# Graph network in two layers on one core: edge counts in groups of two and three chunks instead of four, with Wk on a second queue and the w products moved to the end

## What is computed

```python
edge_index = jnp.stack([src, dst])            # 16384 edges, dst sorted, 1024 nodes, x is 1024x512 f32
h = jnp.maximum(_layernorm(x), 0.0)
# layer 0: attention along edges
q = h @ Wq + bq; k = h @ Wk + bk; v = h @ Wv + bv
adj = jnp.zeros((N, N)).at[src, dst].set(1.0)
a = q @ k.T / sqrt(512);  a = a * adj + (1.0 - adj) * -1e6
x = x + softmax(a) @ v
# layer 1: two aggregations over the edges (with loops), weights from degrees
h = jnp.maximum(_layernorm(x), 0.0)
h = agg(h @ W1 + b1)                          # segment_sum of dinv[src]*dinv[dst]*h[dst] into src
h = relu(gamma * (h - mean) * rsqrt(var + 1e-5) + beta)
x = x + agg(h @ W2 + b2)
```

## The kernel before

| window (in order) | 14 | 15 | 0 | 1 | 2 | 3 | 4 | 5 | 6 | 7 | 8 | 9 | 10 | 11 | 12 | 13 | sum |
|---|---|---|---|---|---|---|---|---|---|---|---|---|---|---|---|---|---|
| first chunk | 119 | 123 | 0 | 32 | 45 | 55 | 64 | 71 | 78 | 85 | 91 | 95 | 101 | 106 | 110 | 115 | |
| chunks touched | 5 | 5 | 33 | 14 | 11 | 10 | 8 | 8 | 8 | 7 | 5 | 7 | 5 | 5 | 6 | 5 | 142 |
| groups of 4, chunks done | 2, 8 | 2, 8 | 9, 36 | 4, 16 | 3, 12 | 3, 12 | 2, 8 | 2, 8 | 2, 8 | 2, 8 | 2, 8 | 2, 8 | 2, 8 | 2, 8 | 2, 8 | 2, 8 | 43, 172 |
| 2 and then threes, chunks done | 5 | 5 | 35 | 14 | 11 | 11 | 8 | 8 | 8 | 8 | 5 | 8 | 5 | 5 | 8 | 5 | 55, 149 |

## Time and profile before

### The profile page before, as it was taken

How to read it: one execution, slowest core, us unless ns; L and a number is a source line. 1 busy time by engine, 2 the same in 40 slices (tenths; PEclk the granted TensorE clock), 3 DMA queues, 4 the chain that set the end, 5 groups by cost and what they waited for, 6 DMA issues and landing times.

```text
span 318.9 us, 4799 instructions
## 1 busy us (share of the span) xinstructions
PE 302.8 (95%) x1358; PEld 234.0 (73%) x1358; DVE 214.7 (67%) x481; ACT 143.5 (45%) x245; POOL 55.8 (17%) x96
## 2 busy tenths in 40 slices
PE   4996999999999799999999999999999999999995
PEld 3874746656757378888888888888788888888884
DVE  4892999999999814796575764748634189367311
ACT  2884973544435453645445456437543024433000
POOL 4395120000000061002214212020210024200000
PEclk9998799999999989999999999999999999999999
DMA  6812320000320030953727154242204000000231
GB/s 232 310 31 82 88 97 34 2 1 0 134 66 0 0 69 0 230 84 83 122 57 154 33 132 80 54 82 49 51 16 67 2 0 2 0 0 1 78 121 66
DMA packets 42309, 21.64 MB, mean 68 GB/s; under 512 B 35760, under 2 KB 36016, under 8 KB 42288
## 3 DMA queue, kind: packets, MB, share of 16 engines
q1 hardware_dynamic: 42288, 21.38, 26.7%
HBM read 10.88 MB, written 2.10 MB: 41 GB/s over the span
## 4 chain that ended last, share of the span: by engine, by line
PE 70%; DVE 11%; issue 5%; POOL 4%; DVEq 3%; ACT 3%; DMA 2%; SPq 1%; ACTq 0%; POOLq 0%
PE ps L936 16%; PE ps L937 16%; PE ps L938 16%; PE ps L1180 9%; PE ps L1103 8%; DVE src_oh L662 5%; PE ps L1011 4%; DMA qk_raw<-L_gnn_Wq_in 2%; POOL drel_second L352 2%; DVEq L662 2%; DVE dst_oh L664 2%; POOL drel_first L352 1%; DVEq L657 1%; ACT T L419 0%; ACT T L425 0%
## 5 line engine op out<-in xcount | busy, mean ns | idle before, releaser
L662 DVE TENSOR_SCALAR src_oh<-iota,ecol 128x512 f16 x172 | 49.1, 345 | 2.6 <-issue 1.6
L1011 PE MATMUL ps<-src_oh,dst_oh 128*128 x172 | 42.1, 385 | 4.6 <-DVE dst_oh L664 4.6
L1011 PEld LDWEIGHTS ps<-src_oh,dst_oh 128*128 x172 | 18.5, 114 | 20.9 <-issue 9.4
L1103 PE MATMUL ps<-cnt,qh 128*128 128x512 f32 x128 | 30.1, 391 | 0.3 <-ACT cnt L532 0.3
L434 ACT ACTIVATE cnt<-ps 64x512 int16<-64x512 f32 x32 | 18.9, 591 | 25.1 <-PE ps L1016 24.7
L1180 PE MATMUL ps<-qh,cnt 128*128 128x512 f32 x128 | 29.3, 390 | 0.0
L1103 PEld LDWEIGHTS ps<-cnt,qh 128*128 128x128 f32 x128 | 23.9, 188 | 5.6 <-DVE qh L815 0.7
L1180 PEld LDWEIGHTS ps<-qh,cnt 128*128 128x128 f32 x128 | 24.0, 188 | 5.2 <-DVE vb L917 0.3
L938 PE MATMUL ps<-v,pT 128*128 128x512 f32 x64 | 25.0, 390 | 0.0
L936 PE MATMUL ps<-hT,qh 128*128 128x512 f32 x64 | 24.9, 389 | 0.0
L937 PE MATMUL ps<-v,pT 128*128 128x512 f32 x64 | 24.9, 389 | 0.0
(11 more groups left out here) (178 smaller groups left out, 667.6 us busy)
## 6 DMA issues: line engine op xcount, KB each, us to landing
xt<-x_in SPq DMA_DIRECT2D x16, 256.0 KB, 3.3
out<-xt SPq DMA_DIRECT2D x8, 256.0 KB, 2.0
qk_raw<-L_gnn_Wk_in SPq DMA_DIRECT2D x2, 512.0 KB, 4.3
qk_raw<-L_gnn_Wq_in SPq DMA_DIRECT2D x2, 512.0 KB, 6.8
wB_raw<-L_gnn_Wv_in SPq DMA_DIRECT2D x2, 512.0 KB, 8.7
wB_raw<-L_gnn_W_in SPq DMA_DIRECT2D x2, 512.0 KB, 3.8
w_raw<-L_gnn_W_in SPq DMA_DIRECT2D x2, 512.0 KB, 4.1
bias_row<-L_gnn_b_in SPq DMA_DIRECT2D x2, 256.0 KB, 3.9
```

The source lines that it names most:

```text
L662: dve.tensor_scalar(src_oh[:, bass.ds(slot, 1), j, :].rearrange("p a n -> p (a n)"), iota[:, :], ecol[:, bass.ds(c + j, 1)], None, ALU.is_ ...
L1011: m = pe.matmul(ps[:, i % 2, :], dst_oh[:, bass.ds(slot, 1), :, j].rearrange("p a n -> p (a n)"), src_oh[:, bass.ds(slot, 1), j, :].rearra ...
L1103: m = pe.matmul(bank(g), qh[:, d, a, c * P:(c + 1) * P], cnt[:, d, n * HALF:(n + 1) * HALF], start=(d == 0 and a == 1), stop=last)
```

## The change

Six edits: (1) a window's counts start with two chunks in a straight line (`LEAD = 2`), whose first matmul begins the bank anew, so that the matmul with zeros at the start goes; (2) the loop then takes three chunks a round (`UNROLL = 3`); (3) POOL does the coefficients of row blocks 2 and 3 right after those of 0 and 1, and the targets of most windows later; (4) ACT issues the two loads of Wk, SP only those of Wq; (5) `columns_of_biases` goes in four parts after i = 6, 7, 8, 9 instead of two; (6) item w is made before the last window, and the w products and `mask_level` come after it.

```diff
-UNROLL = 4
+LEAD = 2
+UNROLL = 3
+PAD = 4
+ROUNDS = NW * (2 + NCH // UNROLL)
...
-             [("q", 0, 1)], [("q", 0, 2), ("w", 0, 0)], [("q", 0, 3)], [], []]
+             [("q", 0, 1)], [("q", 0, 2)], [("q", 0, 3)], [], [("w", 0, 0)]]
...
@@ block.sync
-        for n, (w, name) in enumerate(((Wk, "Wk_in"), (Wq, "Wq_in"))):
...
+        for j in range(LOADS):
+            sp.dma_start(half_of_qk(Q, j), half_in_dram(Wq, j)).then_inc(S[f"Wq_in{j}"], 16)
...
@@ block.gpsimd
-        for i in range(4):
+        for i in range(3):
             targets_of(i)
         ln1(0)
-        for i in range(4, NW):
+        ln1(2)
+        for i in range(3, 8):
             targets_of(i)
-        for t in range(2, NT, 2):
-            ln1(t)
+        ln1(4)
+        ln1(6)
+        for i in range(8, NW):
+            targets_of(i)
...
@@ block.scalar
+        for j in range(LOADS):
+            act.dma_start(half_of_qk(K, j), half_in_dram(Wk, j)).then_inc(S[f"Wk_in{j}"], 16)
...
@@ block.vector
+        def chunks_of(i, c, count):
+
+            k = dve.snap(made, min_val=0, max_val=ROUNDS)
+            slot = k & (RING - 1)
+            dve.wait_ge(S["onehots_used"], k + 1)
+            for j in range(count):
+                dve.tensor_scalar(src_oh[:, bass.ds(slot, 1), j, :].rearrange("p a n -> p (a n)"), iota[:, :],
+                                  ecol[:, bass.ds(c + j, 1)], None, ALU.is_equal)
+            dve.tensor_tensor(dst_oh[:, bass.ds(slot, 1), :, 0:count].rearrange("p a n u -> p (a n) u"),
+                              iota_w[:, :, 0:count],
+                              drel(i)[:, bass.ds(c, count)].rearrange("p (o u) -> p o u", o=1).to_broadcast(
+                                  [P, P, count]), ALU.is_equal).then_inc(S["onehots"], 1)
+            dve.reg_add(made, made, 1)
+
         def onehots(i, bounds):
 
-            first, end = bounds & 255, bounds >> 8
+            first, end = bounds & (NCH - 1), bounds >> 8
             dve.wait_ge(S["drel_ready"], i + 1)
-            with dve.Fori(first, end, UNROLL) as c:
...
+            chunks_of(i, first, LEAD)
+            with dve.Fori(first + LEAD, end, UNROLL) as c:
+                chunks_of(i, c, UNROLL)
...
-            if i == 7:
-                columns_of_biases(K)
-            if i == 9:
-                columns_of_biases(Q)
-            if i == NW - 2:
-                mask_level(slice(0, KC))
+            if 6 <= i <= 9:
+                columns_of_biases(K if i < 8 else Q, (0, 1) if i % 2 == 0 else (2, 3))
         for i in range(NW - 2, NW):
             for item in ahead[i]:
                 lo_of(item)
+        mask_level(slice(0, KC))
...
@@ block.tensor
+        def chunks(i, count, first):
+
+            k = pe.snap(used, min_val=0, max_val=ROUNDS)
+            slot = k & (RING - 1)
+            pe.wait_ge(S["onehots"], k + 1)
+            for j in range(count):
+                m = pe.matmul(ps[:, i % 2, :], dst_oh[:, bass.ds(slot, 1), :, j].rearrange("p a n -> p (a n)"),
+                              src_oh[:, bass.ds(slot, 1), j, :].rearrange("p a n -> p (a n)"), start=first and j == 0,
+                              stop=False, skip_group_check=True)
+            m.then_inc(S["onehots_used"], 1)
+            pe.reg_add(used, used, 1)
+
         def counts(i, bounds):
 
             if i >= 2:
                 pe.wait_ge(S["c16"], 2 * (i - 1))
-            pe.matmul(ps[:, i % 2, 0:32], zerob[:, :], zerob[:, 0:32], start=True, stop=False, skip_group_check=True)
...
+            chunks(i, LEAD, True)
+            with pe.Fori(first + LEAD, end, UNROLL):
+                chunks(i, UNROLL, False)
```

More of the change, by code:

```diff
@@ L101, in gnn_kernel @@
     vb, iota_w, dcol, drel_first = shared([("vb", [P, 2, D], F32)],
-                                    [("iota_w", [P, 2 * WIN, UNROLL], F16), ("dcol", [P, NCH + UNROLL], F16),
-                                     ("drel_first", [P, NW // 2, NCH + UNROLL], F16)])
+                                    [("iota_w", [P, 2 * WIN, UNROLL], F16), ("dcol", [P, NCH + PAD], F16),
+                                     ("drel_first", [P, NW // 2, NCH + PAD], F16)])
     hold("region_vb", 4)
-    p16T, drel_second = shared([("p16T", [P, 2, NT, P], F16)], [("drel_second", [P, NW // 2, NCH + UNROLL], F16)])
+    p16T, drel_second = shared([("p16T", [P, 2, NT, P], F16)], [("drel_second", [P, NW // 2, NCH + PAD], F16)])
     hold("region_p16T", 4)
@@ L109, in gnn_kernel @@
     hold("region_dst_oh", 4)
-    ecol = sb("ecol", [P, NCH + UNROLL], F32)
+    ecol = sb("ecol", [P, NCH + PAD], F32)
     hnT, res, res_h = shared(
@@ L214, in weight_load @@
         return at[:, part, j * k:(j + 1) * k, :]
+    half_of_qk = lambda n, j: qk_raw[:, n, j * KC // LOADS:(j + 1) * KC // LOADS, :]
+    half_in_dram = lambda w, j: w.rearrange("(k p) n -> p k n", p=P)[:, j * KC // LOADS:(j + 1) * KC // LOADS, :]
     ACT_COUNTS, DVE_COUNTS = (0, 1, 2, 3), (4, 5, 6, 7)
@@ L267, in _ @@
         load_w(1)
-        sp.wait_ge(S["uw_ready"], 2)
+        sp.wait_ge(S["uw_ready"], 4)
         sp.dma_start(bias_row[:, 0, :], bv.rearrange("(o n) -> o n", o=1).to_broadcast([P, D])).then_inc(S["bias_in"], 16)
@@ L443, in hi_of @@
                 if item == ("q", 0, 0):
-                    act.wait_ge(S["uw_ready"], 2)
+                    act.wait_ge(S["uw_ready"], 4)
                 if item == ("q", 1, 0):
@@ L669, in columns_of_biases @@
-        def columns_of_biases(n):
-            if n == K:
+            chunks_of(i, first, LEAD)
+            with dve.Fori(first + LEAD, end, UNROLL) as c:
+                chunks_of(i, c, UNROLL)
+        def columns_of_biases(n, ks):
+            if (n, ks) == (K, (0, 1)):
                 dve.wait_ge(S["qk_bias_in"], 32)
-            for k in range(KC):
+            for k in ks:
                 ins = dve.scalar_tensor_tensor(out=qk_raw[:, n, k, :], in0=qk_raw[:, n, k, :], scalar=1.0,
@@ L676, in columns_of_biases @@
                                                accum_out=uw[:, n, k:k + 1])
-            if n == Q:
+            if (n, ks) == (Q, (2, 3)):
                 ins = dve.scalar_tensor_tensor(out=bias_row[:, 0, :], in0=bias_row[:, 0, :], scalar=1.0,
@@ L691, in mask_level @@
             if blocks.start == 0:
-                dve.wait_ge(S["uw_ready"], 2)
+                dve.wait_ge(S["uw_ready"], 4)
                 dve.wait_ge(S["item_lo"], nth(("w", 0, 0)))
@@ L968, in make @@
                 else:
-                    pe.wait_ge(S["uw_ready"], 2)
+                    pe.wait_ge(S["uw_ready"], 4)
                 for k in range(KC):
```

## The result

The changed kernel takes 311.6 us (median of 4, 311.3 to 311.82), the kernel before 320.37 on the same chip (4 runs): 8.8 us less, ratio 0.9727 with a 95% interval of 0.9706 to 0.9747. The forecast was 312.3 us, in a range of 306 to 317. The profiled execution of the changed kernel took 311.82 us, its span is 309.8 us.

The account below looks back on a forecast made before the run. DVE was taken to set the pace of the windows, its sequencer almost as slow as its engine, after a start held up by POOL. -5.8 - 2.2 - 0.4 = -8.4 us against 320.72 gives 312.3 us, range 306 to 317.

Parts of the forecast that it names:

- (a): Start up to DVE's first `src_oh` of w0: POOL's new order ends ACT's wait, 28.8 for 34.62, -5.8 us.
- I take 0, with 1 us either way: At the start, Wk's loads on ACT's queue: Wq maybe up to 1 us earlier, Wk's second half later; counted as 0.
- (b): The windows, from 34.62 to 110.42, where DVE sets the pace: 73.6 us for 75.8, -2.2 us.
- the rows: POOL's eight `drel_second` rows, now in w0 and w1, slow DVE's `src_oh` there: 0.7 us.
- rival (2): In the windows DVE's sequencer doesn't hold DVE back, 68.3 us: total 307.0, range 305 to 309.5; 17%.
- rival (3): In the windows `dst_oh` of three costs 0.47, 3.8 us more: total 316, range 315 to 318; 13%.
- my own rule: A window of r rounds lasts the larger of 1.9 + 1.16 r + 0.1 and 0.75 + 1.13 r + 0.6 per low part.
- rival (4): Each of POOL's eight rows shuts DVE out for its whole 0.74 to 0.78 us: total 316.5 to 318; 4%.
- (c): From 110.42 to `copy_predicated` at 121.81: one chunk less in the last round at the low clock, -0.4 us.
- Rival (5): PE's sparser rounds make the clock fall, 1.8 us each; more than five on the path give over 321.6; 3%.

Follow-up runs that it names:

- e2: The kernel before with POOL's new order alone: 315.68 us, ratio 0.9877.
- e6: The changed kernel with bias columns in two parts again and item w, its products and the mask level back among windows w10 to w13: 312.96 us.
- e5: The changed kernel itself measured once more as a yardstick: 311.36 us, ratio 0.9729 to the kernel before.
- e9: The changed kernel with each `src_oh` only 256 columns wide, with the same instructions on DVE: 308.25 us (a single run).
- e13: The kernel before with the new grouping alone, plus 12 matmuls of zeros on PE before its wait for LayerNorm of blocks 2 and 3: 316.97 us.
- e1: The changed kernel with Wk's two loads back on SP's queue: 311.18 us, ratio 0.9725 to the kernel before.
- e1b: The changed kernel with Wk's loads back on SP, measured again beside the changed kernel: 310.94 us, ratio 0.971 to the kernel before.
- e10: The changed kernel with POOL's `iota_w` moved behind `ident`, `iota` and `half_pow`, Wk still on ACT's queue: 311.72 us.
- e11: The changed kernel with Wk's loads back on SP and POOL's `iota_w` moved behind `ident`: 310.99 us.
- e3: The kernel before with the grouping alone (two chunks in a straight line, rounds of three, no zero matmul at the start): 318.81 us, ratio 0.997.
- e4: The changed kernel with POOL's old order: 318.03 us, ratio 0.994 to the kernel before.

## Why the prediction was right, step by step

**(a), -5.8 forecast, -3.83 found.** POOL's order did what was said: coefficients at 22.77 us, ACT without a wait. Two things ate 2 us. From m(0,0) to the first `src_oh` of w0 it is 17.9 us in all the kernels that have edits 1, 2 and 3 (17.88 to 17.95), where I had 28.8 - 11.41 = 17.4: the gap ahead of `src_oh` is 0.76 to 0.79 us, not 0.5, and the rest is spread. And m(0,0) itself was 1.43 us later in the profiled execution. The step that failed is "I take 0, with 1 us either way" for Wk's queue. I had looked only at Wk and Wq; the loads of the edges are issued beside them on SP and small, and it is the sources of the edges that land 1.4 to 2 us later beside the second queue. Of the 1.43 us, 0.8 is the queue in the mean, the rest varies from run to run with the transposes. In the timed runs the queue costs 0.4 to 0.7 us, inside the "1 us either way".

**(b), -2.2 forecast, -3.4 found.** The runs split the term. POOL's order alone takes it from 75.8 to 75.55 us (e2), the grouping on top of that to 73.84 (e6), bias columns and w products to 72.38 (e5): -0.24, -1.71 and -1.46. POOL's -0.24 is itself two things: the 0.70 us that w0 stands for PE in the kernel before goes away with the low clock, and the `drel_second` rows take 0.47 back. I had the rows, at 0.7, and not the wait; the other two I had at -2.9 together, for -3.17 found.

Rounds come every 1.16 us by the sequencer, as forecast, and rival (2) falls by e9. In the changed kernel's profiled execution `dst_oh` of 384 lasts 0.41 to 0.42 us wherever it begins, so rival (3) falls and with it 0.47 for three. `dst_oh` of 256 lasts 0.36 to 0.39 us in the six windows whose first chunk is even (45.58 above is w1, first chunk 32) and 0.41 to 0.42 in the eight where it is odd (52.88, w2, first chunk 45). This fits the count of four-byte words that I had set against rival (3): 0.36 for one word a row, 0.41 to 0.42 for two, 0.54 for three.

The size that was off: the short windows. I charged 3.1 us to one of 2 and 3 chunks; w8 and w10 take 2.6. For w9 my list has 3.8 us where my own rule gives 1.9 + 2.32 + 0.1 = 4.3; 3.76 were measured. Against 72.9 us without POOL I would have needed 71.9.

Under POOL's rows a round of w0 takes 1.28 for 1.16 us (39.73 to 41.01), four rounds in all. The changeover to w1 hides it on DVE: w0 lasts 14.22 us, as in e13, which has no such rows there. But PE gets w0's last chunks and its next v item 0.5 us later, and DVE then waits 0.65 us for a ring slot in w1 (50.02), which lasts 7.34 us for 6.87 in e13. So the eight rows of 0.71 us cost the path 0.47 us in all, and rival (4), the full block, is out. The Trainium skill ("SBUF — State Buffer", SBUF: two separate sides) says that the other side fully blocks; this trace shows less than a tenth of that on the path.

**(c), -0.4 forecast, -1.84 found.** I assumed the fall of the clock at 110 us again. It came in none of the 13 other profiled executions here. That isn't the change's doing alone: e2 has the very waits of PE before w13's groups that I had read as its reason (1.41 and 0.47 us; the earlier trace rows: 1.42 and 0.47) and (c) is 9.76 us there, 1.64 less. A mean clock of 0.984, that of the profiled execution of before, was seen in 3 of the 23 runs of before in the last group, with a median of 320.79 us; 16 had 0.987 to 0.989, with 320.02. So this part of the 9.07 us depends on which execution was profiled, while the median fell by 8.8. What decides that fall stays open.

**Rival (5).** The clock falls that I feared were in the kernel before: three of its 23 runs, with a clock of 1.0, took 317.67 to 317.93 us, 2.1 to 2.3 below the median. POOL's new order takes away PE's wait near 29 us and so the low clock behind it. It isn't all of it: three of e2's six runs still had 0.993 or 0.994 and took 316.12 to 317.21 us, where the others took 315.06 to 315.25. With the grouping on top (the changed kernel, e1, e1b, e5, e6, e10, e11) all 40 timed runs had 0.998 or more, so sparser rounds brought no low clock. I had booked the order's gain as ACT's 5.8 us of waiting alone; it also guards w0, which would stand 1.9 to 2.2 us for PE in rounds of three (e3, e4).

The errors, -5.8 for -3.8 on one side and -2.6 for -5.2 on the other, nearly cancel. That 312.3 came so close was luck: it is a sum whose terms were off by 2 and 2.6 us.

**The best version** has Wk on SP: 310.9 to 311.2 us (e1, e1b, e11) for 311.4 to 311.7.

## What to carry to other kernels

Before a loop's work is cut, time its rounds on the sequencer: with the `src_oh` half as wide they still came every 1.16 us. When a wait on a side engine leaves TensorE idle just ahead of a stretch in which it must keep up with a ring, count the low clock behind the wait as part of its price; 2.75 us of zeros in that wait bought 1.9 us of the windows. And when a big load goes to a second queue, look at the smallest transfers that are needed first, not at the big ones.

## What was not expected of the hardware

An iota of 128x384 with runs of three took 2.27 us on POOL, the one of 128x512 with runs of four 1.21. The load of the edges' sources (128x128 int32, issued at 1.2 us) was there at 3.1 to 4.4 us beside one queue of weights and at 5.1 to 5.3 beside two. DVE's `dst_oh` with four targets a row costs 0.42 or 0.54 us by the place where it begins, with three 0.41 to 0.42 anywhere, with two 0.36 to 0.39 or 0.41 to 0.42 (the changed kernel's profiled execution).
